# Six results of a token summed in the first expert stage, and ScalarE normalising in the mixing stage

## The reference

```python
x = x + tanh(g_xattn[0]) * attention(layernorm(x), ctx, ctx, ...)   # over the 16 heads of one token
x = x + tanh(g_ffn[0])   * experts16(layernorm(x), ...)             # 6 of 16 experts of 176 hidden, and a shared one
x = x + tanh(g_xattn[1]) * wkv(w, u, layernorm(x), ctx)             # running maximum, numerator and denominator over 64 steps
x = x + tanh(g_ffn[1])   * experts64(layernorm(x), ...)             # 8 of 64 experts of 96 hidden
```

## Time and profile before

| | us |
|---|---|
| three timed runs | 2299.5, 2300.85, 2301.25 (median 2300.85) |
| the profiled execution | 2299.31, of which its span (first to last instruction) 2297.5 |
| stage H0, first matmul to last result | 683.5 to 1218.8 |
| stage M, from the barrier before to the one behind | 1230.5 to 1755.5 |
| stage H1, first matmul to last result | 1759.4 to 2263.8 |
| busy over the span | PE 72%, DVE 58%, POOL 46%, ACT 30% |

### The profile page before, as it was taken

How to read it: one execution, slowest core, us unless ns; L and a number is a source line. 1 busy time by engine, 2 the same in 40 slices (tenths; PEclk the granted TensorE clock), 3 DMA queues, 4 the chain that set the end, 5 groups by cost and what they waited for, 6 DMA issues and landing times. The chain is left out here.

```text
span 2297.5 us, 36021 instructions
## 1 busy us (share of the span) xinstructions
PE 1661.1 (72%) x9250; PEld 1209.0 (53%) x9250; DVE 1335.5 (58%) x3716; ACT 688.2 (30%) x1894; POOL 1051.2 (46%) x1039
## 2 busy tenths in 40 slices
PE   2959984987609999999994433333113999999993
PEld 1437763654307777777772222222113888787872
DVE  5113323666505555555552999999951567777774
ACT  1421221222003333333330322222202555455541
POOL 5022001677743333333331056666674666566662
PEclk9989995998859999999996766666556999999997
DMA  4585736533435576675524344442595668788885
GB/s 145 183 147 71 95 68 225 203 122 113 149 128 187 185 257 207 222 239 189 190 84 144 128 139 159 160 162 96 192 339 171 189 193 268 258 279 275 291 270 180
DMA packets 245364, 419.25 MB, mean 182 GB/s; under 512 B 92097, under 2 KB 176193, under 8 KB 243265
## 3 DMA queue, kind: packets, MB, share of 16 engines
q1 hardware_dynamic: 172336, 215.58, 33.1%
q0 software_dynamic: 48144, 138.57, 16.3%
q10 hardware_dynamic: 24704, 62.98, 7.9%
HBM read 253.36 MB, written 209.88 MB: 202 GB/s over the span
## 5 line engine op out<-in xcount | busy, mean ns | idle before, releaser
L920 PE MATMUL ps<-w_all,h_xT 128*128 x2112 | 547.7, 382 | 5.1 <-ACT h_xT L1143 5.1
L937 PE MATMUL ps<-w_all,h_hT 89*128 (+1 forms) x1472 | 416.2, 387 | 2.5
L663 POOL DMA_INDIRECT y_b<-h_y,h_ix x320 | 316.5, 989 | 203.9 <-DVE h_y L1664 105.9
L646 POOL DMA_INDIRECT xs_b<-h_x,slot_of x256 | 270.9, 1058 | 243.8 <-DVE slot_of L1497 167.9
L920 PEld LDWEIGHTS ps<-w_all,h_xT 128*128 128x128 f32 x2112 | 344.2, 191 | 53.9 <-issue 9.4
L663 POOL DMA_INDIRECT y_a<-h_y,h_ix x208 | 201.3, 968 | 350.8 <-DVE h_y L1664 341.6
L913 PE MATMUL ps<-ident,h_x 128*128 128x128 f32 x1056 | 204.6, 275 | 119.4 <-DMA h_x<-xs_a 63.6
L1664 DVE TENSOR_SCALAR h_y<-ps,h_sum 128x256 f32<-128x256 f32 x528 | 253.5, 480 | 49.0 <-PE ps L937 24.9
L937 PEld LDWEIGHTS ps<-w_all,h_hT 89*128 89x128 f32 (+1 forms) x1472 | 239.1, 191 | 32.5 <-issue 7.1
L1143 ACT COPY h_xT<-ps 128x256 f32<-128x256 f32 x528 | 195.8, 371 | 166.9 <-PE ps L913 148.3
L913 PEld LDWEIGHTS ps<-ident,h_x 128*128 128x128 f32 x1056 | 149.2, 142 | 176.5 <-issue 120.1
(11 more groups left out here) (237 smaller groups left out, 2143.9 us busy)
## 6 DMA issues: line engine op xcount, KB each, us to landing
xs_b<-void_d ACTq DMA_DIRECT2D x40, 1128.0 KB, 13.7
h_x<-xs_b SPq DMA_DIRECT2D x80, 564.0 KB, 7.6
h_x<-xs_a SPq DMA_DIRECT2D x52, 564.0 KB, 4.2
k_a<-y_a SPq DMA_DIRECT2D x16, 1536.0 KB, 7.9
w_all<-in_exp SPq DMA_DIRECT2D x7, 2560.0 KB
h_x<-y_b SPq DMA_DIRECT2D x28, 512.0 KB, 4.7
s_b<-y_b SPq DMA_DIRECT2D x28, 512.0 KB
qkv_d<-a_out ACTq DMA_DIRECT2D x8, 1536.0 KB, 7.5
```

The lines of the kernel that those rows point to most:

```text
L646: pool.indirect_dma_start(xs_d[L.name], bass.IndirectOffsetOnAxis(ap=slot_of[:, g * GT + j, k:k + 1], axis=0), h_x[:, g % NB, j, :], None) ...
L663: pool.indirect_dma_start(y_d[L.name], bass.IndirectOffsetOnAxis(ap=h_ix[:, s:s + 1], axis=0), h_y[:, s % YB, :], None).then_inc(q["y_st"] ...
L920: m = pe.matmul(ps[:, 2 + s % 2, 0:2 * L.H], h_xT[:, s % 2, c, :], w_all[:, bass.ds(e * L.W + c * 2 * L.H, 2 * L.H)], start=(c == 0), stop ...
L937: m = pe.matmul(ps[:, 6 + s % 2, 0:D], h_hT[0:w, s % 2, j, :], w_all[0:w, bass.ds(e * L.W + L.up0 + j * D, D)], start=(j == 0), stop=(j == ...
```

## The change

The sums of the first layer move into H0 for groups 0 to 6, in the manner of H1: a new buffer `h_c` for one token tile, `first_token_in` on SP (one load of 768 KB each, which waits until the tile before has been used), and `first_add_token` on DVE in five parts. The steps are 47, 53, 59, ... (one token tile in six tiles) and for the last group 191, 195, 199, 203. Group 7 is still summed in M, in turn 1 of the loop. In M, ACT applies both normalisations as `Identity` with a scale and a bias from SBUF (`scaled`); DVE makes only the scale 1/std and the bias -mean/std. The roots of groups 0 to 6 are taken at once. The order of the loop changes for DVE, ACT, PE and SP.

```diff
+                def first_add_token(t, part):
+                    if part == 0:
+                        dve.wait_ge(t_in, 16 * t + 16)
+                        dve.tensor_tensor(h_c[:, 0:3 * D], h_c[:, 0:3 * D], h_c[:, 3 * D:6 * D], ALU.add)
+                    elif part == 1:
+                        dve.drain()
+                        dve.tensor_tensor(h_c[:, 0:D], h_c[:, 0:D], h_c[:, D:2 * D], ALU.add)
+                        dve.drain()
+                        dve.tensor_tensor(h_c[:, 0:D], h_c[:, 0:D], h_c[:, 2 * D:3 * D], ALU.add)
+                    elif part == 2:
+                        dve.drain()
+                        dve.scalar_tensor_tensor(x_res[:, t, :], h_c[:, 0:D], tgate[:, 2:3], x_res[:, t, :],
+                                                 ALU.mult, ALU.add).then_inc(t_done, 1)
+                    elif part == 3:
+                        dve.drain()
+                        dve.bn_stats(stats[:, t, :], x_res[:, t, :])
+                    else:
+                        moments_from_stats(t // GT, wk_var if t == NT - GT - 1 else wk_part)
+            def first_token_in(t):
+                if t % GT == 0:
+                    n = tiles_of_groups(L0, t // GT + 1)
+                    for s in range(YB):
+                        sp.wait_ge(lay["a"]["y_st"][s], 16 * ((n - s + YB - 1) // YB))
+                if t:
+                    sp.wait_ge(t_done, t)
+                sp.dma_start(h_c[:], of_tokens(L0)[t // GT, :, t % GT, 0:L0.K * D]).then_inc(t_in, 16)
...
+            def scaled(g, dst):                                   # ACT
+                for j in range(GT):
+                    t = g * GT + j
+                    m = act.activation(dst[:, j, 0:D], x_res[:, t, :], ACT.Identity, bias=mean[:, t:t + 1],
+                                       scale=rstd[:, t:t + 1])
+                return m
+            def scale_of(part):                                   # DVE
+                dve.reciprocal(rstd[:, part], rstd[:, part])
+                dve.drain()
+                return dve.scalar_tensor_tensor(mean[:, part], mean[:, part], -1.0, rstd[:, part], ALU.mult, ALU.mult)
...
                 if g:                                             # ACT's loop
                     deviations(L1, g - 1)
+                    rows_normalised(g - 1)
+                    turned(L1, g - 1)
                 if g < NG:
                     decays(g, 1)
                 if g:
-                    turned(L1, g - 1)
                     exponentials_of(L1, g - 1)
+                if g == 2:
+                    key_deviations(2, slice(NT - GT, NT))
                 if g + 1 < NG:
-                    key_deviations(g + 1)
+                    keys_normalised(g + 1)
                     keys_turned(g + 1)
...
                 if g:                                             # DVE's loop
-                    normalised_rows(L1, g - 1)
+                    row_scales(g - 1)
                 if g < NG:
                     over_time(g, 0)
                 if g:
                     less_largest(L1, g - 1)
-                if g + 1 < NG:
-                    choices_added(g + 1)
+                if g < NG:
+                    over_time(g, 1)
+                if g == 1:
+                    last_choices_added()
                 if g:
                     chosen_experts(L1, g - 1)
-                if g < NG:
-                    over_time(g, 1)
+                if g == 2:
+                    key_scales(2, slice(NT - GT, NT))
                 if g:
                     slots_of(L1, g - 1)
-                if g + 1 < NG:
-                    keys(g + 1)
                 if g < NG:
                     divided(g)
```

More of the change, by code:

```diff
@@ L343, in flamingo @@
         wk_k = sem("wk_k")
-        k_in = [sem(f"k_in{s}") for s in range(2)]
+        k_in = sem("k_in")
         k_done = sem("k_done")
@@ L362, in flamingo, with tiles_of_groups @@
         done = {"a": 0, "b": NG}
[L364 to L370, removed]
+        def tiles_of_groups(L, n):
+            return NTOK // NG * L.K // P * n + L.E - 1
+        sum_at = {"a": {}, "b": {}}
+        for L in (L0, L1):
+            each = NTOK // NG * L.K // P // GT
+            for t in range(NT - GT):
+                ready = tiles_of_groups(L, t // GT + 1) + SUM_ROOM
+                sum_at[L.name][t] = ready + (each if t // GT < NG - 2 else each - 2) * (t % GT)
         halves = [h_x[:, NB - 1].rearrange("p j c -> p (j c)")[:, 0:CHOICES // 2 * D], s_b[:]]
@@ L1731, in _, with last_choices_added, key_scales, row_scales @@
             end_stage(dve, "H0")
-            def choices_added(g):
-                dve.wait_ge(k_done, 2 * g + 2)
+            def last_choices_added():
+                g = NG - 1
+                dve.wait_ge(k_done, 1)
                 dve.scalar_tensor_tensor(group_of(g, x_res), ps[:, 2:4, :].rearrange("p a n -> p (a n)"),
-                                         tgate[:, 2:3], group_of(g, x_res), ALU.mult, ALU.add).then_inc(k_used, 1)
+                                         tgate[:, 2:3], group_of(g, x_res), ALU.mult, ALU.add)
                 dve.drain()
                 moments_of(g, wk_var)
-            def keys(g):
-                part = slice(g * GT, g * GT + GT)
-                dve.wait_ge(wk_std, g + 1)
+            def scale_of(part):
                 dve.reciprocal(rstd[:, part], rstd[:, part])
                 dve.drain()
[L1745 to L1749, removed]
+                return dve.scalar_tensor_tensor(mean[:, part], mean[:, part], -1.0, rstd[:, part], ALU.mult, ALU.mult)
+            def key_scales(n, part):
+                dve.wait_ge(wk_std, n)
+                scale_of(part).then_inc(wk_scale, 1)
+            def row_scales(g):
+                part = slice(g * GT, g * GT + GT)
+                if g >= NB:
+                    dve.wait_ge(lay["b"]["row_st"][g % NB], 16 * GT * L1.K * (g // NB))
+                dve.tensor_copy(h_x[:, g % NB, :, RW - CH1 - 1:RW], tail[:, part, :])
+                dve.wait_ge(g_std, NG + g + 1)
+                scale_of(part).then_inc(g_scale, 1)
             def flat(ap):
@@ L1809, in residual @@
                 moments_of(g)
+            key_scales(1, slice(0, NT - GT))
             no_rows_yet(L1)
```

82 lines of the change are left out of this document (42 added, 40 removed).

## The result

The changed kernel takes 2321.26 us, the median of 4 runs (2318.62 to 2325.56), and the kernel before 2300.18 (4 runs, 2298.6 to 2301.25) beside it: ratio 1.0094, interval 1.0077 to 1.0112. It is 21 us slower, where 2300 was forecast and 2316 was the end of the range. The profiled execution has a span of 2323.7 us.

What follows compares the result with a forecast made beforehand. DVE was taken to bound M, PE H0 until the sums make DVE its bound. H0 +47 and M -47.5 sum to -0.5, giving 2300 us, range 2282 to 2316.

Steps and rivals of the forecast that it cites:

- the load's: H0: each 768 KB load lands in about 5 us, hidden up to step 191; 1 us late three times, 3 us.
- rival (3): H0: single buffer, loads over 8.7 us beside void rows, 1 us wait in each of 18 token tiles: +18, 2318; chance 0.07.
- DVE's work in H0: H0: the sums lengthen the stage by 37 us for 24 token tiles plus 7 for the last four, 44.
- lower bound of 40: H0: 81 us of added DVE work less 41 us of room behind PE, the least H0 grows by.
- Rival (2): H0: no delay absorbed between tiles, token tiles cost 1.9 us each, 56 with the load: +8, 2309; chance 0.20.
- Part 0: H0, DVE: the 768-wide addition of a token tile, priced at 0.96 us, 0.88 in a row.
- M: Stage M: 68.4 us won, less 15.4 and 5.5 of new waits, 47.5 won; bounds 42 to 60.
- The first `exponents`: Start of M: they run 7.0 us behind the barrier instead of 30.3, 23.2 won; bounds 20 to 24.
- wait A: M, turns 1 to 7: DVE's `less_largest` waits 2.2 us a turn for the logits, 15.4; bounds 5 to 18.
- wait B: M, turn 1, once: DVE waits 5.5 us for the 24 matmuls of group 7's sums; bounds 3 to 6.
- just hidden: M: ACT's `decays(g, 1)` ends 8.9 us behind `exponents(g, 1)`, before `over_time(g, 1)` starts at 10.
- four Identity activations at 1.8: M, ScalarE: 0.52 us for one activation alone, some 0.42 in a row, four together 1.8.

Runs made afterwards that it cites:

- e1: Changed kernel with one void-row transfer behind every fourth tile instead of four at the head of 16: 2282.84 us, ratio 0.9925.
- f2: Changed kernel, bursts kept, two buffers for the six results, loads issued a set of four tiles earlier: 2497.78 us against 2535.52 for the kernel before.
- e4: Changed kernel without DVE's additions and statistics in H0, token-tile loads and their waits kept: 2299.08 us in one run.
- f1: Kernel before with only the void-row transfers spread, one behind every fourth tile: 2525.63 us against 2535.52, ratio 0.9966.
- f3: Kernel before with ScalarE's normalisations, void rows spread and only group 0 summed in H0: 2499.42 us against 2535.52, ratio 0.9859.
- g1: Kernel before with ScalarE's normalisations, DVE's M list reordered, void rows spread, only group 0 summed in H0: 2258.94 us, ratio 0.9829.
- g3: Kernel before with ScalarE's normalisations, DVE's M list reordered, void rows spread, groups 0 and 1 summed in H0: 2259.26 us, ratio 0.9825.
- e3: Changed kernel with DVE's `less_largest` moved behind `over_time(g, 1)` in M: 2324.78 us, ratio 1.0107.
- g2: Changed kernel with void rows spread, `less_largest` behind `over_time(g, 1)`, and `decays(g, 1)` ahead of the rows on ScalarE: 2274.82 us, ratio 0.991.
- h1: Kernel before with only the void-row transfers spread, timed a second time: 2479.23 us against 2491.17, ratio 0.9957.
- e6: Kernel before with ScalarE's normalisations and `choices_added`, `over_time(g, 1)` and the keys' scale moved earlier in DVE's M list: 2483.72 us against 2535.52, ratio 0.9798.

## Why the prediction was wrong

**The step that failed** is the load's: "Up to step 191 there are then 3.3 tiles, 8.7 us: hidden." It priced 768 KB at "about 5" from two medians over the whole stage, and allowed 3 us of waits. The time to landing is not one number: it was 4.6 in the median and 18.5 behind a burst, since four transfers of 1128 KB were issued just ahead. The waits came to 29.1: 27.5 of them in five token tiles and not in 18, and 1.7 in the last group, where 3 had been allowed. The bursts stand once in 16 tiles, eight of them while token tiles are loaded. The two loads issued 2 us behind a burst's first issue were waited for 8.8 and 8.3 us, the three issued 8 us behind one 3.2 to 3.7, and the three issued 3 us ahead of one not at all. This is the mechanism of rival (3), a load that outlasts its 8.7 us while the void rows are written, which was given 0.07 and 1 us a token tile. The row against it, tile rows that land in 4.2, was again a median, over loads that mostly don't meet a burst. That the load's timing is the cause is shown from both sides: e1 (bursts apart, loads as late) and f2 (bursts kept, loads early) both remove the waits, and e4 has them without the sums.

**DVE's work in H0**, forecast 44 with a lower bound of 40: 603.3 - 532.8 - 29.1 = 41.4 by the waits, 561.9 - 523.6 = 38.3 by e1 against f1, and f2 gives 34.1 over the kernel before. That is 34 to 41, by profiles that differ by up to 4 us without cause. A token tile costs 1.3 to 1.5 us in f3, g1 and g3, for 1.57; the bound at 40 was no bound. Rival (2), nothing carried over, would have been 56: it is out. Part 0 takes 0.96 as priced, in the row at 920.87.

**M**, forecast 47.5: 45.8. The first `exponents` came 6.3 us behind the barrier for 7.0; wait A was 16.4 in seven turns for 15.4 (8.7 less 6.4 is 2.3 a turn, where the prediction wrote 2.2); wait B 4.9 for 5.5. `decays(g, 1)` was "just hidden" as priced, and e3 showed how just. PE is at its lower level in M, with a granted clock of 0.51 where the kernel before had 0.63 in such a turn, and 8 turns of `h_x` take 1.97 us in it (at 1415.90, say), as in turn 8 before: the matmuls of the removed sums were what stood ahead of these 8 at 2.4 GHz. The Trainium skill ("TensorE: Matmul & The Clock Gate", section "Part 1: The HAM clock gate (the "warmup" mystery)") says that an idle PE drops to 1.2 GHz, and these rows agree. Of wait A's chain one price was low, ScalarE's four Identity activations at 1.8; their timeline in the changed kernel:

```profile
1463.97 2.08 ACT L1211 ACTIVATE h_x<-x_res,mean,rstd 128x256 f32<-128x256 f32 x4 [5.01 <-DVE mean L1792]
```

**The sum.** Forecast -0.5; the load's waits add 29.1 - 3, the work takes off 44 - 41.4, M adds 1.7: +24.7, and H0 and M of the two traces differ by 70.2 - 45.8 = 24.4. One term was mis-sized tenfold, and the others were within 3 us. The 41.4 is what H0 grew by less the waits, so the sum closes in H0 by itself; the 38.3 of e1 against f1 is the reading that doesn't. The range of 2282 to 2316 left the case out because the wait was bounded by another wait's median and not by the worst landing beside a burst.

## What to carry to other kernels

A load that is "hidden" needs its landing time at the place where it is issued, not the median of its group: ask for the transfers of a window around each large burst, above all one on another engine's queue, and for the size of its packets. Spread such bursts, or issue the load a buffer earlier; the one took 41 us out of this stage, the other 36.

Moving work off the bounding engine of one stage onto that of another pays only for the part that stands alone on the path. Here the first group gave three times its cost, the second about its cost, and the six beyond the first cost 32.2 us (H0, e1 against g1) and won 18.6 in M (508.3 in g1, 489.7 in g2), even with both lists reordered.

When a wait is covered by reordering one engine's list, check what its producers have in front of it: e3 turned one wait into another of the same size, and reordering both lists (g2) gave 7 of the 16 us back.

## What the runs showed of the hardware

Three DMA queues with work got equal numbers of packets, and their shares of the bytes went by the size of the packets: 98, 97 and 95 packets from 907 to 917, of 24, 6 and 3 KB. From 1053 to 1063, behind another burst, they were 107, 106 and 100. A small load beside a transfer in large packets got a fifth of the bytes.

A DMA issue on ScalarE's queue takes 0.5 to 0.8 us of its list (four: 0.48 + 1.94), and a compute instruction behind them waits. Taken apart, the bursts made H0 9 us shorter (f1, h1), although ScalarE is busy only 35% of it.

A wait that stopped PE for 8 us left it at its lower level (1.2 GHz, a granted clock of 0.50): in the changed kernel the granted clock is 1.00 from 910 to 915, before the stop, 0.55 in the 5 us from the restart at 923.15, and 1.00 in the next 5.

```profile
923.00:928.00 5.00, 4.85 (x14) 3.45 (x15) 3.41 (x10) 1.05 (x4) 1.59 (x2) 0.55 0.11 38
928.00:933.00 5.00, 5.00 (x26) 3.70 (x25) 3.25 (x9) 1.75 (x6) 1.50 (x2) 1.00 0.80 202
```

The three additions of `h_gu` that follow start at 921.75, 925.03 and 928.28, 3.3 us apart instead of 2.5. How much of that is the clock, and how much the sums between them, no run separates.

The kernel before took 2298 to 2300 us in three groups of runs, and 2536 and 2491 in two others. H0 is equal in them within 2 us, while in f1 the stages ahead of it are 105 us longer, M 51 and what follows M 80, and engines wait there for nothing that the trace names. The cause stays open: the record gives chip 3 both for e1's group (2300.37) and for h1's (2491.17), so different chips alone are not shown to be it. e6 took 2.0% off in such a group and was not timed in a fast one, so a verdict on an edit of M holds for the group in which it was timed.
